# 80 of 100 term scatters moved to the experts' block, and the last score batch with its lane chain placed behind all expert tiles

## The chip, the cores and the metric

The kernel runs as one program on one core of a Trainium2 chip. The metric is the device time of one execution in microseconds. Three executions of the kernel before took 4361.23, 4351.35 and 4353.69 us; the median is 4353.69 us.

## What is computed

A graph layer and a routed expert layer over 12,500 nodes of 256 features, with 212,500 edges sorted by destination and 131,072 further edges for the router's attention. Cut to what matters:

```python
xn = layernorm(x)
x = x + gnn(xn, edges) + linear_attention(xn)         # gnn: mean of xn[src] per dst, then two matrices
h = layernorm(x) @ W_gat                              # 16 terms of each node (4 heads x 4 experts)
e = leaky_relu(a_src[src2] + a_dst[dst2])             # one score per head of each of 131072 edges + loops
ee = exp(e - segment_max(e, dst2)[dst2])
agg = segment_sum(h[src2] * ee / denom, dst2)         # softmax over the edges of a node
w = softmax(top2(mean_heads(layernorm(agg + b_gat)))) # two experts of each node
x = x + sum_e w[e] * (gelu(xn2 @ W1[e] + b1[e]) @ W2[e] + b2[e])
```

`xn2` is the layer norm of the new x. `a_dst`, four terms of each node, is what the moved scatters carry.

## The kernel before, in words

The program is four blocks, one after the other. At a block's end every engine meets the others at a barrier. The order inside a block is written out by hand: each engine has its own loop, and semaphores tie the loops together.

1. Loads of edges and weights.
2. A sort of the router's edges by destination across the 128 lanes (DVE), and the first layer norm beside it.
3. **The graph block** (L646 to L1120). GpSimd (POOL) gathers 128 rows at a time for 1664 chunks of edges (L796), and TensorE sums them by one-hot matrices. Beside it, a software pipeline over 100 tiles of 125 nodes makes the mean, the attention and the second layer norm of each tile, and last `router_row` (L936) copies each tile's router terms into `rt` (stored as `route_rows`) and its four destination terms into `ad_all`. After its last gather POOL scatters `ad_all`, one tile at a time (L799 to L802), into `ad_rows`: the terms of a node go to the place of its first edge.
4. **The experts' block** (L1122 on). TensorE runs 25 groups of 4 tiles: 32 products by W1 for the group into `HP` (L1587), a Gelu on ScalarE into `hid` (L1560), then 16 products by W2 per tile into `Y` (L1595). DVE adds the bias into `y_sb` (L1534), SyncE stores it to `y_rows` (L1223). Two `Y` buffers are in turn, so TensorE waits for DVE at `s_yc` two tiles later.

Beside the tiles runs the edge softmax, in 16 batches of 64 columns of 128 edges. POOL gathers `nb` (source terms, L1270, 64 a batch), at most `AHEAD` = 4 in flight and 3 batch buffers deep. Between two tiles DVE does `scores(b)` (L1309) after tile `unit_after(b)` and `records(b)` (L1334) after the tile behind that; ScalarE takes the exponentials; SyncE stores each batch of running records to `rec_rows` (L1226). Since a node's edges may run over from one lane to the next, the **lane chain** repairs the ends: `lane_ends`, `over_lanes`, `lane_sums`, `first_maxima`, `first_records` (L1355 to L1429). It needs two rounds of transposes on TensorE (L1601, L1606), two exponentials on ScalarE, one gather on POOL (`fix`, L1276, after the last record store) and one scatter back (L1279). The place of each part is a fixed number of tiles behind the last batch:

```python
def unit_after(b):
    t = int((b + 1) * 5.65) + 3
    return t if t % 4 < 2 else t + 4 - t % 4
```

This gives tiles 8, 16, 20, 25, 32, 36, 44, 48, 53, 60, 65, 72, 76, 84, 88 and 93 for the 16 batches, so `LAST` is 93 and the chain's five parts stand after tiles 94 to 98.

The kernel's **tail**: POOL gathers the last record of each node, 100 gathers `res` (L1286). `weigh(k)` makes the gates of 20 tiles on DVE (L1437 on), and `combine(t)` (L1520) sums the four expert rows of a tile, which SyncE has loaded from `y_rows` 8 tiles ahead (`final_loads`, L1240) and stores to `out` (L1250).

Of the kernel before, what the change touches and what calls it, by code (L numbers as in the profile page):

```python
# [8 lines left out]
ACT = mybir.ActivationFunctionType  # L9
# [4 lines left out]
NT = N // NP  # L14
# [33 lines left out]
FT = 20  # L48
FG = NT // FT
AHEAD = 4  # L50
NS = 2 * SPANS
MIX_AT = NT + 3
HISTS = FC // 8
# [66 lines left out]

def unit_after(b):

    t = int((b + 1) * 5.65) + 3
    return t if t % 4 < 2 else t + 4 - t % 4


def build(nc, x, src, dst, gnn_w, gnn_b, wqkv, wkv_t, wout_t, bout, w_gat, att_src, att_dst,
          b_gat, ln_g, ln_b, w1, b1, w2, b2, fedge, out):
    ctx = ExitStack()
    with ctx:  # L130
# [515 lines left out]
        with ExitStack() as stage, nc.Block() as block:  # L646
# [141 lines left out]
            @block.gpsimd  # L788
            def _(pool):
                nc.gpsimd.iota(spare[:], [[1, NP]], base=EF, channel_multiplier=NP, allow_small_or_imprecise_dtypes=True).then_inc(s_sp, 1)  # L790

                for s in range(NS):
                    g, h, w = s // 2, s % 2, s // 2 % 2
                    pool.wait_ge(s_used[h], g + 1)
                    for q in range(HU):
                        pool.indirect_dma_start(out=rows[w][h][:, q, 0:D], out_offset=None, in_=xn_rows,  # L796
                                                in_offset=bass.IndirectOffsetOnAxis(ap=gsrc[:, s * HU + q:s * HU + q + 1], axis=0)
                                                ).then_inc(s_rows[w][(h * HU + q) // QUAD], 16)
                for t in range(NT):  # L799
# [322 lines left out]
        with ExitStack() as stage, nc.Block() as block:  # L1122
# [78 lines left out]
            LAST = unit_after(NB - 1)  # L1201
            assert LAST + 4 < NT and LAST // 4 == NG - 2

            @block.sync
            def _(sp):
                for to, of in ((b1_sb[:], b1), (b2_b[:], row_of(b2.rearrange("e f -> (e f)"), NE * D)), (bg[:], row_of(b_gat, 16)),
                               (lg[:], row_of(ln_g, 16)), (lb[:], row_of(ln_b, 16))):
                    sp.dma_start(to, of).then_inc(s_pl, 16)

                def load_group(g):  # L1210
                    u = g % 2
                    if g >= 2:
                        sp.wait_ge(s_hp, (g - 1) * 16)
                    for i in range(4):
                        sp.dma_start(x2g[u][:, :, i, :], x2_turned[4 * g + i].rearrange("p (k n) -> p k n", k=2)).then_inc(s_x2l[u], 16)

                load_group(0)
                load_group(1)
                sp.wait_ge(s_ads, 16 * NT)
                sp.dma_start(ad[:], ad_rows[0:EF, :].rearrange("(p f) h -> p f h", p=P)).then_inc(s_adl, 16)  # L1220
                for t in range(NT):
                    sp.wait_ge(s_yc, t + 1)
                    sp.dma_start(y_rows[t], y_sb[t % 2][:]).then_inc(s_ys[t % 2], 16)  # L1223
                    for b in batches_after(t - 2):
                        sp.wait_ge(s_rec, b + 1)
                        sp.dma_start(rec_rows[0:EF, :].rearrange("(p f) c -> p f c", p=P)[:, b * W:(b + 1) * W, :],  # L1226
                                     rec[b % 2][:]).then_inc(s_recs[b % 2], 16)
                    if t % 4 == 0 and t // 4 + 2 < NG:
                        load_group(t // 4 + 2)

                def final_loads(t):
                    q = t % YR
                    if t % FT == 0:
                        k = t // FT
                        if k >= 2:
                            sp.wait_ge(s_mrg, k - 1)
                        sp.dma_start(own[k % 2][:], route_rows[t * NP:(t + FT) * NP, :].rearrange("(t p) c -> p t c", p=NP)).then_inc(s_own, 16)
                    if t >= YR:
                        sp.wait_ge(s_acc, t - YR + 1)
                    sp.dma_start(y_in[q], y_rows[t]).then_inc(s_yl[q], 16)  # L1240
                    sp.dma_start(x1_in[q], x1_rows[t]).then_inc(s_yl[q], 16)  # L1241

                sp.wait_ge(s_y, NT)
                for u in range(2):
                    sp.wait_ge(s_ys[u], 16 * NT // 2)
                for t in range(YR):
                    final_loads(t)
                for t in range(NT):
                    sp.wait_ge(s_acc, t + 1)
                    sp.dma_start(out[t * NP:(t + 1) * NP, :], acc[t % AR][:]).then_inc(s_out[t % AR], 16)  # L1250
                    if t + YR < NT:
                        final_loads(t + YR)
                for q in range(AR):
                    sp.wait_ge(s_out[q], 16 * NT // AR)

            @block.gpsimd
            def _(pool):
                nc.gpsimd.memset(first_e[:], 1.0).then_inc(s_fe, 1)
                pool.wait_ge(s_fe, 1)
                nc.gpsimd.affine_select(out=first_e[:], in_=first_e[:], compare_op=ALU.is_gt, fill=0.0, base=0,  # L1260
                                        pattern=[[1, 4], [-1, 4]], channel_multiplier=0).then_inc(s_fe, 1)
                pool.indirect_dma_start(out=ad_first[:], out_offset=None, in_=route_rows,
                                        in_offset=bass.IndirectOffsetOnAxis(ap=first_i[:, 0:1], axis=0)).then_inc(s_adf, 16)
                for b in range(NB):
# [25 lines left out]
            def _(dve):  # L1290
# [238 lines left out]
                for t in range(NT):  # L1529
                    dve.wait_ge(s_y, t + 1)  # L1530
                    if t >= 2:
                        dve.wait_ge(s_ys[t % 2], (t // 2) * 16)
                    for half in range(2):
                        last = v.tensor_tensor(y_sb[t % 2][0:NP, half * 512:half * 512 + 512], Y[t % 2][half][0:NP, :],  # L1534
                                               b2_b[:, half * 512:half * 512 + 512], ALU.add)
                    last.then_inc(s_yc, 1)
                    if t == unit_after(0) - 3:
                        start_ad()
                    for b in batches_after(t - 1):
                        records(b)  # L1540
                    for b in batches_after(t):
                        scores(b)
                    for part, at in ((lane_ends, 1), (over_lanes, 2), (lane_sums, 3), (first_maxima, 4), (first_records, 5)):
                        if t == LAST + at:
                            part()
                for k in range(FG):
                    weigh(k)
                    for t in range(k * FT, (k + 1) * FT):
# [3 lines left out]
            def _(act):  # L1552
                a = nc.scalar.activation
                act.wait_ge(s_pl, 5 * 16)
                for g in range(NG):
                    for c in range(16):
                        act.wait_ge(s_hp, g * 16 + c + 1)
                        if g:
                            act.wait_ge(s_y, g * 4)
                        a(hid[:, c, :], HP[c % 4][:, 0:4 * NP], ACT.Gelu, bias=b1_sb[:, c:c + 1]).then_inc(s_hid, 1)  # L1560
                    for j in range(4):
                        for b in batches_after(4 * g + j):
                            act.wait_ge(s_dif, b + 1)
                            a(dd[:], dd[:], ACT.Exp).then_inc(s_ex, 1)
                    if g == LAST // 4:
                        act.wait_ge(s_endd, 1)
                        a(dc[:], dc[:], ACT.Exp).then_inc(s_ende, 1)
# [11 lines left out]
            def _(pe):  # L1579
                mm = nc.tensor.matmul  # L1580
                def group(g, u, pair):
# [9 lines left out]
                    for j in range(4):  # L1591
# [6 lines left out]
                        if isinstance(g, int) and 4 * g + j == LAST + 2:  # L1598
                            pe.wait_ge(s_ends, 1)
                            for k in range(4):  # L1600
                                last = nc.tensor.transpose(HP[0][0:20, k * P:(k + 1) * P], ends[:, k, :], ident)  # L1601
                            last.then_inc(s_endt, 1)
                            pe.wait_ge(s_endc, 1)
                        if isinstance(g, int) and 4 * g + j == LAST + 3:
                            pe.wait_ge(s_fx, 1)
                            nc.tensor.transpose(HP[1][:, 0:20], fm[:, 0:P], ident[0:20, 0:20])  # L1606
                            nc.tensor.transpose(HP[1][:, 20:40], fx[:, 0:P], ident[0:20, 0:20]).then_inc(s_back, 1)

                for g in range(2):
                    group(g, g, 0)  # L1610
# [2 lines left out]
                        group(i * 2 + (2 + u), u, i + 1)  # L1613
                for g in range(NG - 3, NG):
                    group(g, g % 2, g // 2)


_INS = ["x", "src", "dst", "L0_gnn_weight", "L0_gnn_bias", "L0_mix_Wqkv", "kv_turned", "out_turned", "L0_mix_bout",
# [26 lines left out]
```

## Time and profile before

| | us |
|---|---|
| median of three executions | 4353.69 |
| lowest and highest | 4351.35, 4361.23 |
| the profiled execution, first to last instruction | 4353.6 |
| first instruction of the experts' block | 2548.7 |
| first gather of final records (`res`) | 3961.8 |

The profiled execution has no time of its own beside its span; the span lies 0.1 us from the median of the runs, so differences in it are differences of the metric.

| engine | busy us | share of the span |
|---|---|---|
| TensorE, products | 3225.6 | 74% |
| GpSimd | 2900.5 | 67% |
| VectorE | 2057.2 | 47% |
| ScalarE | 831.1 | 19% |

How to read it: a share is an average over four blocks with different limits. The table says who is busy, and only the waits inside a stage say what ends it. A time in a stage is read as the distance between two starts in the timeline, and the rows that are used stand in the section of rows.

### The profile page before, as it was taken

What the parts mean: (1) busy time and instruction counts of PE and PEld (TensorE: products, weight loads), DVE (VectorE), ACT (ScalarE), POOL (GpSimd) and SP (SyncE); (2) the same over time, 40 slices, a digit from 0 to 9 for tenths busy, and PEclk for the clock granted to TensorE, in tenths of its full rate; (3) what the DMA queues carried; (4) which work ended last, traced back from release to release, by engine and by line L of the source; (5) the groups of instructions that cost most, each with busy time, mean ns of one, the idle gap of its engine ahead of it and who ended that gap; (6) DMA issues with size and microseconds to landing.
All of it is one profiled execution on the core that took longest, in us unless ns stands there. A gap on an engine that the chain in (4) does not pass through costs nothing. (4 is left out here: it accounts for less than half of the span.)

```text
span 4353.6 us, 47649 instructions
## 1 busy us (share of the span) xinstructions
PE 3225.6 (74%) x12938; PEld 2167.4 (50%) x12938; DVE 2057.2 (47%) x4751; ACT 831.1 (19%) x2082; POOL 2900.5 (67%) x3009
## 2 busy tenths in 40 slices
PE   0118999999997788888888449999999999993000
PEld 0105666665655565555555326666666666662000
DVE  7885656555655465555455202122223223233677
ACT  4301222222221011111111112222222222221000
POOL 1617777777777777777777767777777777754210
PEclk6559999999999899998999779999999999997555
DMA  6205555555554577666666322222222222223766
GB/s 205 88 31 133 138 137 138 136 138 135 138 137 138 138 182 193 178 177 178 174 180 177 72 55 60 67 69 67 69 62 74 67 67 73 67 66 122 217 208 218
DMA packets 378974, 540.08 MB, mean 124 GB/s; under 512 B 117914, under 2 KB 295418, under 8 KB 378743
## 3 DMA queue, kind: packets, MB, share of 16 engines
q0 software_dynamic: 119136, 234.44, 23.8%
q1 hardware_dynamic: 259735, 304.59, 21.9%
q14 instruction: 78, 0.64, 0.0%
q8 instruction: 25, 0.41, 0.0%
HBM read 392.03 MB, written 146.74 MB: 124 GB/s over the span
## 5 line engine op out<-in xcount | busy, mean ns | idle before, releaser
L796 POOL DMA_INDIRECT rows<-xn_rows,gsrc x1664 | 1578.4, 949 | 507.5 <-issue 506.9
L1270 POOL DMA_INDIRECT nb<-route_rows,idx x1024 | 1014.9, 991 | 318.9 <-issue 302.9
L1024 PE MATMUL PS<-rows,oh 128*128 128x257 f32 x3328 | 884.6, 414 | 277.2 <-DMA rows<-xn_rows,gsrc 276.0
L1024 PEld LDWEIGHTS PS<-rows,oh 128*128 128x128 f32 x3328 | 645.7, 203 | 434.4 <-DMA rows<-xn_rows,gsrc 327.9
L1587 PE MATMUL PS<-x2g,arena 128*128 128x500 f32 x1600 | 678.4, 585 | 95.9 <-DMA x2g<-x_turned 94.1
L1595 PE MATMUL PS<-arena,hid 128*125 128x256 f32 x3200 | 697.5, 380 | 20.8 <-ACT hid L1560 20.8
L1595 PEld LDWEIGHTS PS<-arena,hid 128*125 128x125 f32 x3200 | 598.6, 188 | 129.4 <-issue 33.1
L1534 DVE TENSOR_TENSOR y_sb<-PS,b_b 125x512 f32<-125x512 f32 x200 | 128.6, 685 | 1058.1 <-PE PS L1595 1057.7
L1587 PEld LDWEIGHTS PS<-x2g,arena 128*128 128x128 f32 x1600 | 305.2, 191 | 455.0 <-issue 357.2
L1560 ACT ACTIVATE hid<-PS,b_sb 128x500 f32<-128x500 f32 x400 | 270.8, 677 | 615.8 <-PE PS L1587 615.8
L836 DVE TENSOR_TENSOR oh<-PS,rel 128x1024 f32<-128x1024 f32 x208 | 253.9, 1221 | 11.0
L849 DVE TENSOR_REDUCE ss<-sq 125x16 f32<-125x1024 f32 x100 | 122.0, 1220 | 250.7 <-ACT sq L974 250.7
L1096 PE MATMUL PS<-own_w,p_t 128*125 128x512 f32 x400 | 222.7, 640 | 10.5 <-ACT s_t L984 10.5
L629 PE MATMUL PS<-wide,arena 128*128 128x128 f32 x112 | 27.6, 428 | 248.9 <-DVE arena L545 203.5
L1041 PE MATMUL PS<-arena,x_t 128*125 128x512 f32 x400 | 193.2, 605 | 0.0
L1043 PE MATMUL PS<-arena,x_t 128*125 128x512 f32 x400 | 188.0, 592 | 0.0
L1286 POOL DMA_INDIRECT res<-rec_rows,end_i x100 | 98.7, 987 | 111.2 <-DVE q L1454 80.1
L866 DVE TENSOR_TENSOR oh_lo<-PS,arena 128x500 bf16<-128x500 f32 x256 | 170.9, 667 | 0.0
L866 DVE TENSOR_TENSOR oh_hi<-PS,arena 128x400 bf16<-128x400 f32 x256 | 144.4, 564 | 53.2 <-PE PS L1059 52.9
L973 ACT ACTIVATE sq<-PS 125x512 f32<-125x512 f32 x100 | 59.7, 597 | 540.3 <-PE PS L1043 540.3
L441 POOL TENSOR_SCALAR space<-space,nm,rs 128x256 f32<-128x256 f32 x98 | 104.5, 1083 | 84.5 <-DVE rs L512 84.5
L1520 DVE SCALAR_TENSOR_TENSOR acc<-arena,gate,acc 125x256 f32<-125x256 f32 x300 | 145.5, 485 | 24.3 <-issue 2.2
(300 smaller groups left out, 3122.5 us busy)
## 6 DMA issues: line engine op xcount, KB each, us to landing
y_rows<-y_sb SPq DMA_DIRECT2D x100, 512.0 KB, 2.7
arena<-y_rows SPq DMA_DIRECT2D x100, 512.0 KB, 5.0
rows<-xn_rows,gsrc POOLq DMA_INDIRECT x1664
nb<-route_rows,idx POOLq DMA_INDIRECT x1024
sum_rows<-kept SPq DMA_DIRECT2D x104, 128.5 KB
x_rows<-x SPq DMA_DIRECT2D x100, 128.0 KB, 4.8
hid<-x_rows SPq DMA_DIRECT2D x100, 128.0 KB, 8.3
m_in<-sum_rows SPq DMA_DIRECT2D x100, 125.5 KB
```

The costliest lines, as they stand in the source:

```text
L796: pool.indirect_dma_start(out=rows[w][h][:, q, 0:D], out_offset=None, in_=xn_rows, in_offset=bass.IndirectOffsetOnAxis(ap=gsrc[:, s * HU + ...
L836: v.tensor_tensor(oh[w][h][:], NUMBERS.rearrange("p (o n) -> p o n", o=1).broadcast_to([P, HU, P]), along(rel[h][:], P), ALU.is_equal).the ...
L866: last = v.tensor_tensor(to[:, 4 * h:4 * h + 4, :], NUMBERS[:, 0:n].rearrange("p (o n) -> p o n", o=1).broadcast_to([P, 4, n]), along(of[: ...
L1024: last = mm(SUM[:, 0:D + 1], oh[w][h][:, q, :], rows[w][h][:, q, :], start=h == 0 and q == 0, stop=h == 1 and q == HU - 1)
L1041: mm(KP[0:NP, :], x_t[u][:, k * NP:(k + 1) * NP], wkv[:, k, 0:INNER], start=k == 0, stop=k == 1)
L1043: last = mm(VP[u][0:NP, :], x_t[u][:, k * NP:(k + 1) * NP], wkv[:, k, INNER:2 * INNER], start=k == 0, stop=k == 1)
L1096: both = lambda k: mm(GM[u][0:NP, :], p_t[q][:, k * NP:(k + 1) * NP], own_w[:, k, :], start=k == 0, stop=k == 1)
L1270: pool.indirect_dma_start(out=nb[b % NBUF][:, c, :], out_offset=None, in_=route_rows, in_offset=bass.IndirectOffsetOnAxis(ap=idx[:, b * W ...
L1520: last = v.scalar_tensor_tensor(out=acc[t % AR][:], in0=y_in[q][0:NP, e * D:(e + 1) * D], scalar=gate[:, t, e:e + 1], in1=acc[t % AR][:] i ...
L1560: a(hid[:, c, :], HP[c % 4][:, 0:4 * NP], ACT.Gelu, bias=b1_sb[:, c:c + 1]).then_inc(s_hid, 1)
L1587: last = mm(HP[c % 4][:, 0:4 * NP], w1_sb[:, k, e, (c % 4) * P:(c % 4 + 1) * P], x2g[u][:, k, :, :].rearrange("p j n -> p (j n)"), start=k ...
L1595: last = mm(Y[j % 2][e // 2][0:NP, (e % 2) * D:(e % 2 + 1) * D], hid[:, 4 * e + k, j * NP:(j + 1) * NP], w2_sb[:, e, k, :], start=k == 0, ...
```

## The change

Three things change together.

The scatters are split at `ADS_EARLY` = 20: 20 stay in the graph block, 80 go to the front of POOL's program in the experts' block, ahead of `ad_first` and of all `nb` gathers. SyncE's load of `ad`, which needs all 100, moves from before tile 0 to behind the store of tile 6. `start_ad` goes by `unit_after(0) - 3`, from tile 5 to tile 9.

`unit_after` gives tiles 12, 17, 24, 29, 36, 41, 48, 53, 60, 68, 72, 80, 84, 92, 96 and 100: the last batch stands behind all tiles, and is called `late`.

The lane chain follows the late batch with nothing between its parts, on DVE, ScalarE and TensorE. SyncE stores the late records behind the first eight `final_loads`.

```diff
+ADS_EARLY = 20
 def unit_after(b):
-    t = int((b + 1) * 5.65) + 3
-    return t if t % 4 < 2 else t + 4 - t % 4
+    t = int((b + 1) * 6.06 + 5.5)
+    t = t if t % 4 < 2 else t + 4 - t % 4
+    return min(t, NT)
...
-                for t in range(NT):
+                for t in range(ADS_EARLY):
                     pool.wait_ge(s_hc, t + 2)
                     pool.indirect_dma_start(out=ad_rows, ...)
...
-                sp.wait_ge(s_ads, 16 * NT)
-                sp.dma_start(ad[:], ad_rows[0:EF, :]...).then_inc(s_adl, 16)
                 for t in range(NT):
                     sp.wait_ge(s_yc, t + 1)
                     sp.dma_start(y_rows[t], y_sb[t % 2][:]).then_inc(s_ys[t % 2], 16)
                     for b in batches_after(t - 2):
+                        store_records(b)
+                    if t == 6:
+                        sp.wait_ge(s_ads, 16 * NT)
+                        sp.dma_start(ad[:], ad_rows[0:EF, :]...).then_inc(s_adl, 16)
...
                 for t in range(YR):
                     final_loads(t)
+                for b in late:
+                    store_records(b)
...
+                for t in range(ADS_EARLY, NT):
+                    pool.indirect_dma_start(out=ad_rows, ...).then_inc(s_ads, 16)
                 pool.indirect_dma_start(out=ad_first[:], ...)
...
-                    for part, at in ((lane_ends, 1), (over_lanes, 2), ...):
-                        if t == LAST + at:
-                            part()
+                for b in late:
+                    scores(b)
+                    records(b)
+                lane_ends()
+                over_lanes()
+                lane_sums()
+                first_maxima()
+                first_records()
```

ScalarE's exponentials and TensorE's transposes of the chain move behind the last group in the same way.

How POOL's program reads at the boundary of the two blocks (`ad_rows` are the scatters, `nb` the gathers of source terms), before:

```order
L796 DMA rows<-xn_rows,gsrc 128x256 x7
L801 DMA ad_rows<-ad_all,start_i 143872x4 [waits s_hc] x100
L646 UNCONDITIONAL_BRANCH
L1256 UNCONDITIONAL_BRANCH [waits barrier_Pool_Activation_PE_DVE_SP_gather]
L1258 MEMSET first_e 125x16
L1260 AFFINE_SELECT first_e<-first_e 125x16 [waits s_fe]
L1262 DMA ad_first<-route_rows,first_i 128x28
L1270 DMA nb<-route_rows,idx 128x28 x4
```

and in the changed kernel:

```order
L798 DMA rows<-xn_rows,gsrc 128x256 x7
L803 DMA ad_rows<-ad_all,start_i 143872x4 [waits s_hc] x20
L648 UNCONDITIONAL_BRANCH
L1265 UNCONDITIONAL_BRANCH [waits barrier_Pool_Activation_PE_DVE_SP_gather]
L1267 MEMSET first_e 125x16
L1269 AFFINE_SELECT first_e<-first_e 125x16 [waits s_fe]
L1272 DMA ad_rows<-ad_all,start_i 143872x4 x80
L1274 DMA ad_first<-route_rows,first_i 128x28
L1282 DMA nb<-route_rows,idx 128x28 x4
```

Of the 100 scatters ahead of the barrier 20 are left, and 80 stand between the barrier and the first gather of the batches.

TensorE's program at the lane chain (`x2g` rows are products by W1, `hid` rows products by W2, `ends`, `fm` and `fx` the chain's transposes), before:

```order
L1595 MATMUL PS<-arena,hid 125x256 [waits s_yc]
L1595 MATMUL PS<-arena,hid 125x256 x15
L1601 MATMUL PS<-wide,ends 20x128 [waits s_ends]
L1601 MATMUL PS<-wide,ends 20x128 x3
L1587 MATMUL PS<-x2g,arena 128x500 [waits s_hid,s_x2l0,s_endc]
L1587 MATMUL PS<-x2g,arena 128x500
...
L1595 MATMUL PS<-arena,hid 125x256 [waits s_yc,s_hid]
L1595 MATMUL PS<-arena,hid 125x256 x15
L1606 MATMUL PS<-wide,fm 128x20 [waits s_fx]
L1607 MATMUL PS<-wide,fx 128x20
L1595 MATMUL PS<-arena,hid 125x256 [waits s_yc]
```

and the end of the changed kernel's:

```order
L1614 MATMUL PS<-arena,hid 125x256 [waits s_yc]
L1614 MATMUL PS<-arena,hid 125x256 x15
L1614 MATMUL PS<-arena,hid 125x256 [waits s_yc]
L1614 MATMUL PS<-arena,hid 125x256 x15
L1627 MATMUL PS<-wide,ends 20x128 [waits s_ends]
L1627 MATMUL PS<-wide,ends 20x128 x3
L1631 MATMUL PS<-wide,fm 128x20 [waits s_fx,s_endc]
L1632 MATMUL PS<-wide,fx 128x20
```

The two rounds of transposes stood between groups and tiles of the experts, with waits on the chain's semaphores. Now nothing of the experts stands behind them.

SyncE's program behind the last tiles (`y_rows<-y_sb` stores a tile, `arena<-y_rows` and `hid<-x_rows` are the final loads), before:

```order
L1223 DMA y_rows<-y_sb 128x1024 [waits s_yc] x5
L1226 DMA rec_rows<-rec 128x1536 [waits s_rec]
L1223 DMA y_rows<-y_sb 128x1024 [waits s_yc] x4
L1237 DMA own<-route_rows 125x20x28 [waits s_ys1,s_ys0,s_y]
L1240 DMA arena<-y_rows 128x1024
L1241 DMA hid<-x_rows 128x256
L1240 DMA arena<-y_rows 128x1024
```

and in the changed kernel:

```order
L1224 DMA rec_rows<-rec 128x1536 [waits s_rec]
L1229 DMA y_rows<-y_sb 128x1024 [waits s_yc]
L1244 DMA own<-route_rows 125x20x28 [waits s_ys1,s_ys0,s_y]
L1247 DMA arena<-y_rows 128x1024
L1248 DMA hid<-x_rows 128x256
...
L1247 DMA arena<-y_rows 128x1024
L1248 DMA hid<-x_rows 128x256
L1224 DMA rec_rows<-rec 128x1536 [waits s_rec]
L1259 DMA out<-acc 125x256 [waits s_acc]
```

The last store of records has moved from between the tile stores to behind 17 loads.

## Rows read from the trace of the kernel before

**Rows 1.** A stretch at the end of the graph block; PE, PEld, DVE, ACT, POOL busy, clock, DMA, GB/s.

```profile
2480.00:2500.00 20.00, 0.00 (x0) 0.00 (x0) 0.00 (x0) 0.00 (x0) 15.23 (x16) 0.50 0.03 2
```

**Rows 2.** The scatters, line L801: duration ns min/median/max, first and last start.

```profile
L801 POOL DMA_INDIRECT ad_rows<-ad_all,start_i x100: 965/970/1147, 2411.9 to 2538.3; - x100
```

**Rows 3.** Timeline across the experts' barrier: start, duration, engine, what, [idle before].

```profile
2538.30 0.97 POOL L801 DMA_INDIRECT ad_rows<-ad_all,start_i  x1 [0.30 <-issue]
2548.74 0.11 POOL L1258 MEMSET first_e<- 125x16 f32 x1 [9.47 <-POOLq L646]
...
2560.03 2.87 PE L1587 MATMUL PS<-x2g,arena 128*128 128x500 f32 x3 [94.12 <-DMA x2g<-x_turned]
```

**Rows 4.** Waits of SyncE's queue: total us, times, longest.

```profile
SPq L646 <- PEq L646: 80.3, 1, 80.3
```

**Rows 5.** Timeline across the barrier ahead of the graph block.

```profile
324.05 0.16 DVE L586 TENSOR_TENSOR lane<-lane 128x1 f32<-128x1 f32 x1
...
325.51 0.25 POOL L790 IOTA spare<- 100x125 f32 x1 [86.23 <-POOLq L381]
```

**Rows 6.** The gathers of source terms, line L1270, whole block.

```profile
L1270 POOL DMA_INDIRECT nb<-route_rows,idx x1024: 939/945/4119, 2550.8 to 3883.4; - x171
```

**Rows 7.** POOL's waits from 2549 to 2600 us.

```profile
POOL nb L1270 <- DMA nb<-route_rows,idx: 5.2, 3, 2.8
```

**Rows 8.** SyncE's queue: last record store, first and last of the 17 first final loads.

```profile
3903.40 0.43 SPq L1226 DMA_DIRECT2D rec_rows<-rec  x1
...
3968.26 0.29 SPq L1237 DMA_DIRECT2D own<-route_rows  x1
...
3981.87 0.43 SPq L1241 DMA_DIRECT2D hid<-x_rows  x1
```

**Rows 9.** The first 20 gathers of final records, beside those loads.

```profile
DMA to landing us min/median/max: 2.4/4.5/6.6
```

**Rows 10.** DVE's timeline from the last batch to the end of the lane chain.

```profile
3885.93 0.17 DVE L1316 COPY m_run<-m_run 128x4 f32<-128x4 f32 x1 [3.52 <-DMA nb<-route_rows,idx]
...
3894.93 5.32 DVE L1349 TENSOR_TENSOR_SCAN rec<-dd,rec,msg 128x64 f32<-128x64 f32 x20
...
3902.93 0.67 DVE L1379 COPY endt<-PS 20x512 f32<-20x512 f32 x1
...
3906.38 0.28 DVE L1394 TENSOR_SCALAR dc<-dc 20x256 f32<-20x256 f32 x1
...
3941.93 0.27 DVE L1398 TENSOR_TENSOR dc<-dc,endt 20x128 f32<-20x128 f32 x1
...
3951.59 0.19 DVE L1405 COPY back<-PS 128x40 f32<-128x40 f32 x1
...
3953.26 0.17 DVE L1420 TENSOR_TENSOR d<-z 128x8 f32<-128x8 f32 x1
...
3958.49 0.17 DVE L1426 TENSOR_TENSOR fix<-fix,d 128x20 f32<-128x20 f32 x1
```

**Rows 11.** TensorE's timeline: the chain's two rounds of transposes.

```profile
3900.81 1.03 PE L1601 MATMUL PS<-wide,ends 128*20 128x128 f32 x4 [5.91 <-DVE ends L1363]
...
3942.95 0.23 PE L1606 MATMUL PS<-wide,fm 20*128 20x20 f32 x1 [2.26 <-DVE fx L1401]
```

**Rows 12.** POOL's timeline behind its last gather of source terms.

```profile
3908.32 0.95 POOL L1276 DMA_INDIRECT fix<-rec_rows,fix_i  x1 [23.99 <-DMA rec_rows<-rec]
3959.29 0.99 POOL L1279 DMA_INDIRECT rec_rows<-fix,put_i  x1 [50.02 <-DVE fix L1429]
3961.81 0.97 POOL L1286 DMA_INDIRECT res<-rec_rows,end_i  x1 [1.53 <-DMA rec_rows<-fix,put_i]
```

**Rows 13.** DVE's timeline: the first instruction of the tail.

```profile
3990.77 0.24 DVE L1437 TENSOR_TENSOR zf<-res,own 125x80 f32<-125x80 f32 x1 [25.28 <-DMA res<-rec_rows,end_i]
```

**Rows 14.** The chain that ended last, one group of tiles: start us, us, what.

```profile
2617.18 26.84 PE PS L1587 x64
2644.77 27.89 PE PS L1595 x128
```

More of the change, by code:

```diff
@@ L1200, in build @@
             batches_after = lambda t: [b for b in range(NB) if unit_after(b) == t]
-            LAST = unit_after(NB - 1)
-            assert LAST + 4 < NT and LAST // 4 == NG - 2
+            late = batches_after(NT)
+            assert len(late) == 1
             @block.sync
@@ L1218, in _, with store_records @@
                 load_group(1)
-                sp.wait_ge(s_ads, 16 * NT)
-                sp.dma_start(ad[:], ad_rows[0:EF, :].rearrange("(p f) h -> p f h", p=P)).then_inc(s_adl, 16)
+                def store_records(b):
+                    sp.wait_ge(s_rec, b + 1)
+                    sp.dma_start(rec_rows[0:EF, :].rearrange("(p f) c -> p f c", p=P)[:, b * W:(b + 1) * W, :],
+                                 rec[b % 2][:]).then_inc(s_recs[b % 2], 16)
                 for t in range(NT):
@@ L1224, in _ @@
                     for b in batches_after(t - 2):
-                        sp.wait_ge(s_rec, b + 1)
-                        sp.dma_start(rec_rows[0:EF, :].rearrange("(p f) c -> p f c", p=P)[:, b * W:(b + 1) * W, :],
-                                     rec[b % 2][:]).then_inc(s_recs[b % 2], 16)
+                        store_records(b)
+                    if t == 6:
+                        sp.wait_ge(s_ads, 16 * NT)
+                        sp.dma_start(ad[:], ad_rows[0:EF, :].rearrange("(p f) h -> p f h", p=P)).then_inc(s_adl, 16)
                     if t % 4 == 0 and t // 4 + 2 < NG:
@@ L1261, in _ @@
                                         pattern=[[1, 4], [-1, 4]], channel_multiplier=0).then_inc(s_fe, 1)
+                for t in range(ADS_EARLY, NT):
+                    pool.indirect_dma_start(out=ad_rows, out_offset=bass.IndirectOffsetOnAxis(ap=start_i[:, t:t + 1], axis=0),
+                                            in_=ad_all[:, t, :], in_offset=None).then_inc(s_ads, 16)
                 pool.indirect_dma_start(out=ad_first[:], out_offset=None, in_=route_rows,
@@ L1542, in _ @@
                         scores(b)
-                    for part, at in ((lane_ends, 1), (over_lanes, 2), (lane_sums, 3), (first_maxima, 4), (first_records, 5)):
-                        if t == LAST + at:
-                            part()
+                for b in late:
[6 more added lines that the diff above has]
+                first_records()
                 for k in range(FG):
@@ L1564, in _ @@
                             a(dd[:], dd[:], ACT.Exp).then_inc(s_ex, 1)
-                    if g == LAST // 4:
-                        act.wait_ge(s_endd, 1)
-                        a(dc[:], dc[:], ACT.Exp).then_inc(s_ende, 1)
+                for b in late:
+                    act.wait_ge(s_dif, b + 1)
+                    a(dd[:], dd[:], ACT.Exp).then_inc(s_ex, 1)
+                act.wait_ge(s_endd, 1)
+                a(dc[:], dc[:], ACT.Exp).then_inc(s_ende, 1)
                 act.wait_ge(s_fixd, 1)
@@ L1597, in group @@
                         last.then_inc(s_y, 1)
[L1598 to L1607, printed above, removed]
                 for g in range(2):
@@ L1615, in _ @@
                     group(g, g % 2, g // 2)
+                pe.wait_ge(s_ends, 1)
+                for k in range(4):
+                    last = nc.tensor.transpose(HP[0][0:20, k * P:(k + 1) * P], ends[:, k, :], ident)
+                last.then_inc(s_endt, 1)
+                pe.wait_ge(s_endc, 1)
+                pe.wait_ge(s_fx, 1)
+                nc.tensor.transpose(HP[1][:, 0:20], fm[:, 0:P], ident[0:20, 0:20])
+                nc.tensor.transpose(HP[1][:, 20:40], fx[:, 0:P], ident[0:20, 0:20]).then_inc(s_back, 1)
 _INS = ["x", "src", "dst", "L0_gnn_weight", "L0_gnn_bias", "L0_mix_Wqkv", "kv_turned", "out_turned", "L0_mix_bout",
```

## The prediction, made before the run

> **What bounds the kernel now.** I read the stretch by stretch table first, then the timelines at the seams, and last the waits. Three stages matter.
>
> The end of the graph block: from 2480 to 2500 us only GpSimd works [rows 1]. The 100 scatters, 2411.9 to 2538.3 [rows 2], end that block alone, and the next block's first instruction starts at 2548.74 [rows 3]. SyncE had arrived and waited 80.3 us at the barrier [rows 4]: it was ready at 2548.7 - 80.3 = 2468.4.
>
> The experts' block: two engines run nearly equal courses. TensorE takes 26.84 us and 27.89 us for the two halves of a group, and the halves start 27.56 apart [rows 14], so a group takes 55.6 us and 25 of them some 1390. GpSimd's 1024 gathers start from 2550.8 to 3883.4 [rows 6]. The last batch lands at 3885.93 [rows 10], so the course is 1.30 us a gather and 83.4 a batch. The first gather of final records is at 3961.81 [rows 12]. Of the 75.9 us between, most is no work: GpSimd waits 50.02 us for the end of the lane chain [rows 12], whose parts wait in VectorE's order for tiles 95 to 98.
>
> The tail, from 3961.81 to 4353.6, is 391.8 us. It starts with the final records, so it moves with them.
>
> **The change part by part.** Each term is what it adds to the time at which the final records can be gathered.
>
> 1. *The block starts earlier.* Of 100 scatters 20 stay: from 2411.9 at 1.277 us each (126.4 us over 99 steps [rows 2]) they end at 2437, long before SyncE's 2468.4. SyncE then ends the block. What does the barrier cost? Across the barrier before the graph block, the last VectorE instruction ends at 324.21 and GpSimd starts at 325.51 [rows 5]: 1.3 us. At the experts' barrier there are 9.5 us between the last scatter's end and the start [rows 3]. I take 1.3, since in both cases the late engine is then not GpSimd with scatters just issued, and GpSimd's own 9.5 us would be over by 2447. The block starts at 2469.7 instead of 2548.74: **-79.0**. With the other price it is -70.8; that end is kept.
>
> 2. *80 scatters stand ahead of the gathers.* 80 x 1.277 = **+102.1**. They wait for nothing: the terms have been in `ad_all` since the graph block. Queued behind them are `ad_first` and all gathers, and behind those VectorE's batches. The new table has been set for that: batch b has landed 104.2 + 83.4(b+1) us into the block, for batch 7 at 771; its scores stand after tile 53, which ends at 11.3 (first product at 2560.03 [rows 3]) + 13 x 55.6 + 28 + 14 = 776 [rows 14]. The even places have 20 us or more. So VectorE does not stand waiting with a `Y` buffer in hand. The load of `ad` behind tile 6 (about 117 us into the block) finds the scatters landed at about 107. No term. A batch buffer is free three batches later as before: no term.
>
> 3. *Start-up waits.* The first gathers waited 5.2 us [rows 7] beside the block's first loads. Scatters don't wait for landings; the 2 MB load of `ad` now meets gathers later, for some 2 us. **-3**, between -5.2 and 0.
>
> 4. *The final loads now run beside the last gathers.* TensorE no longer stops for the chain (5.91 + 2.26 us of waits and 1.3 of transposes [rows 11], some 10), so the loads, first issued at 3968.26 [rows 8], start at 3968.3 - 79.0 - 10 = 3879. The 17 are issued in 13.6 us, and their 5 MB need about 26 at the 200 GB/s that the tail moves on the page. The last gather lands near 3908, so 22 gathers or so run beside them. Before, the first gathers of final records ran beside these loads and landed in 2.4 / 4.5 / 6.6 us [rows 9]. With four in flight and 1.25 us apart, a landing up to 5.0 us costs nothing; 6.6 makes it 1.7 us a gather, +10 for the 22. I take **+2**, nearest to the median row, and keep 0 and +10.
>
> The trace has just this pairing in rows 9, so the sum goes by it. The Trainium skill (DMA: Bandwidth & Descriptors, Queues, rings and completion order) says that each DMA engine goes round robin between its queue rows and changes only after a whole packet. By that rule every gather waits behind packets of the loads, which speaks for the +10 and not for the +2; the largest landing agrees with it, the median doesn't decide.
>
> 5. *The chain has nothing between its parts.* From the rows: last landing to the end of the record scans 3900.25 - 3885.93 = 14.3, less 0.6 for a tile's bias that stood in it, 13.7 [rows 10]; to the end of the transposes at 3901.84, 1.6 [rows 11]; `endt` copy to the lane differences 3902.93 to 3906.66, 3.7 [rows 10]; an exponential (0.5, an estimate) and the sums with transposes 3941.93 to 3943.18, 1.8 together [rows 10, 11]; `first_maxima` 3951.59 to 3953.43, 1.85 [rows 10]; an exponential of 0.3 and `first_records` up to GpSimd's scatter, 3958.49 to 3959.29, 0.8 [rows 10, 12]; scatter to first gather 2.5 [rows 12]. Together 26.3, with handovers 27. Before it was 75.9: **-48.9**. The other branch, record store then `fix` gather, takes 4.9 us from the store's issue at 3903.40 [rows 8] to the gather at 3908.32 [rows 12], and 2.4 for a landing [rows 9], 7.3; VectorE needs it 8 us after the scans, so it is covered by under a microsecond, if SyncE is past its 17 loads (issued by 3893, needed at 3922). TensorE's transposes now come after idle time at the low clock; that is 1.03 us of work [rows 11], at most +1.5.
>
> 6. *The tail.* The first `weigh` started 28.96 us after the first gather, since the 20th landed late beside the loads [rows 9, 12, 13]. Now the loads are over; 19 x 1.25 + 2.4 = 26.2: **-2.8**. Behind it the transfers set the pace as before: 0.
>
> Sum: -79.0 + 102.1 - 3 + 2 - 48.9 - 2.8 = **-29.6**. From the execution's 4353.6 that is **4324.0 us**; its span lies 0.1 from the median of the runs, so no correction. The two big gains are bought with the scatters: what is won is the exposed boundary and the slack in the chain.
>
> **The rivals.** A measurement here tells 0.2%, 8.7 us, from no change.
>
> *A: the boundary keeps its 9.5 us* because it is a price of this barrier and not of the scatters. For it: it is the only row of this barrier. Against: rows 5. 4324.0 + 8.2 = 4332.
>
> *B: the last gathers crawl beside the loads.* +8 over my term: 4332; still faster. A and B together, with landings above 6.6 us, 4324 + 8.2 + 14 = 4346: within 0.2%.
>
> *C: the chain doesn't shrink.* Its place is between the last landing and the first final record. If its steps are bound by latencies that overlapped with tiles in the trace (table loads, the record store behind 17 loads, handovers), the 75.9 us stay, and the sum is -29.6 + 48.9 = +19.3: 4373, slower. It decides from a chain of 27 + 29.6 = 57 us; slower by over 0.2% from 65. Against it: 34 us of it are one wait of VectorE for a tile, between the end at 3906.66 and the tile's bias ahead of 3941.93 [rows 10].
>
> *D: the block doesn't start earlier*, since another engine holds the barrier: +79, 4403. Rows 4 nearly exclude it.
>
> **How the numbers follow.** My forecast 0.58; A alone 0.16; B alone 0.10; A and B with slow landings 0.08; C 0.07; D 0.01. Faster 0.58 + 0.16 + 0.10 = 0.84; same 0.08; slower 0.07 + 0.01 = 0.08. The range goes from 4314 (start-up waits gone, B's term 0, the chain 5 shorter) to 4342 (A with B), and leaves out C, D and A with slow landings, 0.16.
>
> **What would show it.** The experts' block starts near 2470 and GpSimd's 80 scatters take 102 us. The last gather lands near 3908, 34 us behind TensorE's last product. The final records start 27 us after it, near 3935. The tail is 389 us. Wrong would be: a start near 2478 (A), waits of `nb` for landings behind the last tile (B), a chain above 35 us (C), or waits of VectorE for `nb` between tiles that push TensorE past GpSimd.

## The result, and the profile after

The changed kernel takes 4322.17 us (4316.73 to 4324.76), the kernel before 4353.69 (4351.35 to 4361.23). The ratio is 0.9927, with a 95% interval of 0.9914 to 0.9939: faster by 0.7%. The prediction was 4324.0 us, in a range of 4314 to 4342. The profiled execution took 4322.32 us with a span of 4320.5, so 33.1 us of span are gone; the times of its stages are used below. In every execution on record that has both, the time is 1.7 to 1.9 us above the span. So the profiled execution before, with its span of 4353.6, took some 4355.4 us and not the median, and the forecast of 4324.0, summed up from that span, is a span too: as a time it is 4325.8.

| us, profiled execution | before | after | predicted |
|---|---|---|---|
| first instruction of the experts' block | 2548.74 | 2464.08 | 2469.7 |
| last batch landed | 3885.93 | 3905.94 | 3908 |
| landing to first final record | 75.9 | 26.4 | 27 |
| first final record | 3961.81 | 3932.29 | 3935 |
| from there to the end | 391.8 | 388.2 | 389 |

First the seam of the two blocks, which answers to [rows 3]: the timeline from 2461 us on; the columns are start, duration, engine, line, what, and the idle time before it. SyncE's wait at the barrier, which answers to [rows 4], stands behind it.

```profile
2461.69 0.16 DVE L945 COPY rt<-PS 125x8 f32<-125x8 f32 x1
2464.08 0.11 POOL L1267 MEMSET first_e<- 125x16 f32 x1 [24.36 <-POOLq L648]
...
2464.79 0.99 POOL L1272 DMA_INDIRECT ad_rows<-ad_all,start_i  x1 [0.30 <-issue]
```

```profile
SPq L648 <- PEq L648: 0.2, 1, 0.2
```

GpSimd now waits 24.36 us at the barrier, and VectorE with SyncE behind it ends the block: VectorE's last instruction ends at 2461.85, SyncE waits only 0.2 us, and the next block starts 2.2 us after VectorE's end. Then come the 80 scatters and the gathers (the rows of lines L1272 and L1282; durations in ns, first and last start):

```profile
L1272 POOL DMA_INDIRECT ad_rows<-ad_all,start_i x80: 968/972/990, 2464.8 to 2565.6; - x80
```

```profile
L1282 POOL DMA_INDIRECT nb<-route_rows,idx x1024: 942/947/3502, 2568.2 to 3903.5; - x171
...
  issue: 302.3, 990
  DMA nb<-route_rows,idx: 19.5, 34
```

From the first scatter to `ad_first` at 2566.90 it is 102.1 us, and no wait is among them. The end of the batches, the chain and the start of the tail, in order of time, answer to [rows 8, 10, 11, 12]:

```profile
3865.33 1.29 DVE L1546 TENSOR_TENSOR y_sb<-PS,b_b 125x512 f32<-125x512 f32 x2 [3.69 <-PE PS L1614]
...
3869.38 0.29 SPq L1244 DMA_DIRECT2D own<-route_rows  x1
...
3905.94 0.17 DVE L1328 COPY m_run<-m_run 128x4 f32<-128x4 f32 x1 [39.33 <-DMA nb<-route_rows,idx]
...
3914.20 5.32 DVE L1361 TENSOR_TENSOR_SCAN rec<-dd,rec,msg 128x64 f32<-128x64 f32 x20
3919.55 0.32 SPq L1224 DMA_DIRECT2D rec_rows<-rec  x1
...
3920.08 1.03 PE L1627 MATMUL PS<-wide,ends 128*20 128x128 f32 x4 [54.79 <-DVE ends L1375]
...
3921.14 0.68 DVE L1391 COPY endt<-PS 20x512 f32<-20x512 f32 x1
...
3923.53 1.27 POOL L1288 DMA_INDIRECT fix<-rec_rows,fix_i  x1 [19.05 <-DMA rec_rows<-rec]
...
3925.39 0.28 DVE L1410 TENSOR_TENSOR dc<-dc,endt 20x128 f32<-20x128 f32 x1 [0.48 <-ACT dc L1586]
```

VectorE has nothing to do for 39.33 us ahead of the last batch, and after it the chain runs with no wait of VectorE above 0.6 us. The waits of GpSimd in the stretch from 3900 us to the tail:

```profile
POOL fix L1288 <- DMA rec_rows<-rec: 19.1, 1, 19.1
...
POOL rec_rows L1291 <- DVE fix L1441: 5.0, 1, 5.0
POOL res L1298 <- DMA rec_rows<-fix,put_i: 1.4, 1, 1.4
```

The 50.02 us that it waited for `fix` in [rows 12] are 5.0 now. In those 5.0 us VectorE is still at work on the sums, so its branch, and not the `fix` gather, is the one that ends last.

### The profile page after: what moved, and what is told of

Read it like the earlier page. It is cut to its first block and busy times, and to the rows that moved or that the text cites. A ratio compares the mean times of both kernels' runs of the same rounds, so it can differ in the third digit from the quotient of the medians.

```text
span 4320.5 us, 47644 instructions
## 1 busy us (share of the span) xinstructions
PE 3219.4 (75%) x12936; PEld 2165.2 (50%) x12938; DVE 2063.0 (48%) x4751; ACT 826.0 (19%) x2078; POOL 2904.4 (67%) x3009
## 5 line engine op out<-in xcount | busy, mean ns | idle before, releaser
L1282 POOL DMA_INDIRECT nb<-route_rows,idx x1024 | 1014.8, 991 | 321.8 <-issue 302.3
L1614 PEld LDWEIGHTS PS<-arena,hid 128*125 128x125 f32 x3200 | 598.6, 188 | 129.5 <-issue 33.1
```

Source lines behind the costliest of these rows:

```text
L1282: pool.indirect_dma_start(out=nb[b % NBUF][:, c, :], out_offset=None, in_=route_rows, in_offset=bass.IndirectOffsetOnAxis(ap=idx[:, b * W ...
```

## The experiments

Each edit is against the changed kernel, where not said otherwise. A time is the median of the runs, a ratio is to the kernel before on the same chip. Each edit of `ADS_EARLY` alone keeps the new table of places.

**The new chain without the moved scatters.** All 100 scatters stay ahead of the barrier.

```diff
-ADS_EARLY = 20
+ADS_EARLY = 100
```

> The changed kernel with all 100 scatters back in the graph block; the new table, the late batch and the chain behind all tiles stay. Theory P (GpSimd's course and the last tile, whichever ends later, set the chain's start): the experts' block starts at 2548.7 as before, its last gather lands 1339.8 us later at 3888.5 (3905.94 - 2568.20 + 2.1 by the changed kernel's trace), but the last tile's bias ends 1402.5 us into the block, at 3951.2. The chain takes 26 us from there and its record store now runs behind and beside the final loads, some 10 more; the tail is 388. Time 4366 to 4376, slower than before by 12 to 22 us. Rival Q (the close-packed chain is a gain of its own, 49 us, wherever the scatters stand): 4353.7 - 48.9 = 4305.

Measured: 4378.34 us, ratio 1.006 (1.0043 to 1.0077), slower than before. GpSimd and VectorE around the block's end, the last batch and the chain (the timeline):

```profile
2539.89 0.97 POOL L803 DMA_INDIRECT ad_rows<-ad_all,start_i  x1 [0.30 <-issue]
2550.33 0.11 POOL L1267 MEMSET first_e<- 125x16 f32 x1 [9.47 <-POOLq L648]
...
3953.57 0.16 DVE L1328 COPY m_run<-m_run 128x4 f32<-128x4 f32 x1
...
3980.89 0.94 POOL L1288 DMA_INDIRECT fix<-rec_rows,fix_i  x1 [94.29 <-DMA rec_rows<-rec]
...
3985.77 1.00 POOL L1291 DMA_INDIRECT rec_rows<-fix,put_i  x1 [3.94 <-DVE fix L1441]
3988.21 0.97 POOL L1298 DMA_INDIRECT res<-rec_rows,end_i  x1 [1.45 <-DMA rec_rows<-fix,put_i]
```

GpSimd's last `nb` gather is at 3885.4, and then the batch lies for some 66 us until the last tile is through VectorE, since its place is behind all tiles. The first final record comes 1437.9 us into the block, where it came after 1413.1 in the kernel before. So the late places and the late chain by themselves cost 0.6%, and the time lies above the 4366 to 4376 expected. They pay only if the gathers end late in the block; no run here has the new table and the close chain apart, so their shares stay open.

**The moved scatters without the new places and chain.** The kernel before, split at 20, with the load of `ad` behind the store of tile 4.

```diff
-                for t in range(NT):
+                for t in range(ADS_EARLY):
...
+                for t in range(ADS_EARLY, NT):
+                    pool.indirect_dma_start(out=ad_rows, ...)
```

> The kernel before with the 80 scatters moved and nothing else, save that the load of ad stands behind the store of tile 4 (its first user comes at tile 5). Theory P: block starts at 2464, the last gather lands at 3906 as in the changed kernel, VectorE stands waiting for every batch and holds the tiles back, so the chain keeps its 75.9 us behind the last landing: final records at 3982, tail 389 to 392, time 4371 to 4374, slower than before by 17 to 20 us. Rival R (the earlier start is the gain, and the scatters' place hides itself): at least -79 + 26 and so 4322 or less.

Measured: 4373.3 us, ratio 1.005 (1.0033 to 1.0067). The block started at 2459.4, and yet it was slower. The waits from 2600 to 3990 us (in all, times, longest):

```profile
DVE m_run L1321 <- DMA nb<-route_rows,idx: 115.0, 9, 23.9
POOL rec_rows L1284 <- DVE fix L1434: 50.7, 1, 50.7
...
PE PS L1600 <- DVE y_sb L1539: 44.8, 3, 28.0
...
DVE m_run L1324 <- DMA nb<-route_rows,idx: 34.0, 1, 34.0
```

VectorE stands at 10 of its 16 places before the batch has landed (the wait for the first batch has a row of its own, 34.0 us), TensorE then runs out of `Y` buffers, and the chain keeps its 50.7 us. Neither half of the change gains; the 0.7% come from both together.

**All scatters behind the barrier.**

```diff
-ADS_EARLY = 20
+ADS_EARLY = 0
```

> The changed kernel with all 100 scatters in the experts' block. Theory P: block starts at 2460 to 2466, the last gather lands 20 x 1.277 = 25.5 us later than in the changed kernel; VectorE now waits 15 to 21 us for each batch at an odd place (tiles 17, 29, 41, 53), which pushes the last tile from 3867 to some 3888, still before the last landing at 3931. Time 4322.2 + 25.5 = 4347.7. Rival S (GpSimd's course does not set the end): 4322 if transfers do, about 4343 if the tiles do and their push of 21 us counts.

Measured: 4346.58 us, ratio 0.9989 (0.9979 to 0.9998). Each of the 20 scatters is worth 24.4 / 20 = 1.22 us against the changed kernel. VectorE waited for `nb` at five places, from 2600 us on, and 2.8 us more at the first batch:

```profile
DVE m_run L1328 <- DMA nb<-route_rows,idx: 99.1, 5, 50.7
```

Of these 99.1 us, 50.7 are the last place; the other four push the tiles 13 us later (the last bias ends 1415.9 us into the block, in the changed kernel 1402.5). That costs nothing, since the bias is done at 3875.0 and the last batch lands at 3925.7.

**30 scatters ahead of the barrier.**

```diff
-ADS_EARLY = 20
+ADS_EARLY = 30
```

> The changed kernel with 30 scatters in the graph block and 70 in the experts' block. Theory P: 30 scatters end at 2414.3 + 30 x 1.277 = 2452.6, and with 9.5 us on top at 2462.1, still before the others' 2461.9 to 2464; the block starts at 2464, the last gather lands 12.8 us earlier, at 3893.2, still 26 behind the last tile. Time 4322.2 - 12.8 = 4309.4. Rival S (the tiles or the final transfers set the end of the changed kernel): no change from 4322.

Measured: 4311.18 us, ratio 0.9906 (0.9889 to 0.9922), 11 us less than the changed kernel for 10 scatters; 12.8 was expected. In the profiled executions the last batch lands 1431.2 us into the block instead of 1441.9, and the chain takes the same 26.4 us. So it is GpSimd's course of scatters and gathers that sets the end here.

**46 scatters ahead.**

```diff
-ADS_EARLY = 20
+ADS_EARLY = 46
```

> The changed kernel with 46 scatters in the graph block. They end at 2414.3 + 46 x 1.277 = 2473.0, after all others, so GpSimd holds the barrier. If the barrier then costs 9.5 us as before (price of scatters just issued): start 2482.5, last landing 2482.5 + 1408.7 = 3891.2, last tile 3885, time 4307. If it costs 1.3 us (the 9.5 was something else): start 2474.3, last landing 3883.0, last tile 3876.8, time 4299. Rival S (end not set by GpSimd's course): 4322 or later, by the later start of the tiles 4333 to 4341.

Measured: 4304.48 us, ratio 0.9892 (0.9875 to 0.9908). GpSimd is the last at the barrier again, and SyncE waits 15.9 us there. The price is neither 1.3 nor 9.5:

```profile
2467.57 0.97 POOL L803 DMA_INDIRECT ad_rows<-ad_all,start_i  x1 [0.30 <-issue]
2474.91 0.11 POOL L1267 MEMSET first_e<- 125x16 f32 x1 [6.37 <-POOLq L648]
...
2475.19 0.91 DVE L1537 MEMSET y_sb<- 128x1024 f32 x1 [18.47 <-PEq L648]
...
3895.16 0.43 SPq L1224 DMA_DIRECT2D rec_rows<-rec  x1
...
3905.53 0.94 POOL L1288 DMA_INDIRECT fix<-rec_rows,fix_i  x1 [31.44 <-DMA rec_rows<-rec]
```

The tiles' course is now as late as the gathers': the last bias starts at 3876.9, the scores at 3878.15 without a wait, and the chain takes 34.8 us instead of 26.4. The interval overlaps with that of 30 scatters, so the two are not told apart.

**Is the block end's price the landing of scatters?** The kernel before, with a wait for all scatters and a mark behind it.

```diff
                     pool.indirect_dma_start(out=ad_rows, ...).then_inc(s_ads, 16)
+                pool.wait_ge(s_ads, 16 * NT)
+                nc.gpsimd.memset(spare[:, 0:1], 0.0)
```

> The kernel before, with a wait of GpSimd for the landing of all 100 scatters at the end of the graph block, and a one-column memset behind it as a mark. Asks what the 9.5 us between the last scatter and the experts' block are. Theory L (they are the scatters' landing, which the barrier waits for anyhow): the mark stands where the landing is, near 2547, and the block starts 1.3 us behind it. Theory G (an end-of-block price of GpSimd after it has issued transfers, not their landing): the mark stands 2 to 3 us after the last scatter, near 2541.5, and the block starts 6 to 8 us behind the mark; time 4352 to 4355, no change. A third way: the wait lets that price run out beside it, block start near 2543, time 4346 to 4348.

Measured: 4353.69 us, ratio 1.0003 (0.9994 to 1.0013). The timeline at the mark:

```profile
2537.33 0.10 POOL L804 MEMSET spare<- 100x1 f32 x1 [1.19 <-DMA ad_rows<-ad_all,start_i]
2546.90 0.11 POOL L1260 MEMSET first_e<- 125x16 f32 x1 [9.47 <-POOLq L646]
...
2547.18 0.91 DVE L1527 MEMSET y_sb<- 128x1024 f32 x1 [91.67 <-PEq L646]
```

The last scatter has landed before the mark at 2537.33, and the 9.47 us begin behind it all the same. So it is no wait for the scatters' data: it belongs to the end of GpSimd's part of the block.

**What sets that price?** Two kernels of one execution each, with 72 and with 54 scatters ahead.

```diff
-ADS_EARLY = 20
+ADS_EARLY = 72
```

> The change with ADS_EARLY = 72, one look at the barrier: what sets the time from GpSimd's last scatter to the next block? It was 9.47 with 100 scatters (before, e1) and 6.37 with 46 (e4). Theory W (it grows with the number of GpSimd's instructions left in the stretch that it works alone): straight between them, 6.37 + 26/54 x 3.1 = 7.9. Rival X (two levels, 9.47 once the other engines have sat idle long enough, 6.37 before): 9.47 or 6.37. Block start near 2410 + 71 x 1.277 + 1 + 7.9 = 2509.6; time about 4304 + 33 = 4337 to 4342.

```diff
-ADS_EARLY = 20
+ADS_EARLY = 54
```

> The same with ADS_EARLY = 54, the second point. Theory W: 6.37 + 8/54 x 3.1 = 6.8. Rival X: 9.47 or 6.37. Block start near 2410 + 53 x 1.277 + 1 + 6.8 = 2485.5; time about 4304 + 10 = 4314.

Measured, with 72: 4341.32 us; with 54: 4318.07 us. The barrier's waits with 72, then with 54:

```profile
DVE y_sb L1537 <- PEq L648: 46.6, 1, 46.6
...
POOL first_e L1267 <- POOLq L648: 8.5, 1, 8.5
```

```profile
DVE y_sb L1537 <- PEq L648: 28.3, 1, 28.3
...
POOL first_e L1267 <- POOLq L648: 7.3, 1, 7.3
```

With 46, 54, 72 and 100 scatters the price is 6.37, 7.32, 8.49 and 9.47 us. Two levels are excluded. It grows, by 0.12 us a scatter at first and 0.04 at last, so a straight line is not right either. VectorE waited 18.5, 28.3, 46.6 and 82.8 us beside it, so in these four alone the price could as well go by the time that GpSimd works alone. Two pairs with the same number of scatters tell the two apart. The last run below has 46 again, and VectorE waited 7 us less there:

```profile
2473.99 0.11 POOL L1267 MEMSET first_e<- 125x16 f32 x1 [6.37 <-POOLq L648]
...
2474.28 0.91 DVE L1537 MEMSET y_sb<- 128x1024 f32 x1 [11.58 <-PEq L648]
```

The price is 6.37 us in both. With 100 scatters VectorE waited 81.3, 82.8 and 91.7 us (the new chain alone, the kernel before, the landing wait), and the price is 9.47 us in all three. So it goes with the number of scatters ahead of the barrier or with what grows in step with it, such as the time since the last gather, and not with the time that the other engines wait; by which mechanism stays open.

**38 scatters ahead.**

```diff
-ADS_EARLY = 20
+ADS_EARLY = 38
```

> The change with ADS_EARLY = 38. Times by the number left behind: 0: 4346.6, 20: 4322.2, 30: 4311.2, 46: 4304.5. Theory P: each scatter is worth 1.28 us until GpSimd itself holds the barrier, 6.4 us behind its last scatter (e4); 38 scatters end at 2410 + 48.5 = 2458.5, plus 6.4 is 2465, so the barrier is still free of them, and the gathers come 8 x 1.277 = 10.2 us earlier than with 30: 4301, unless the last tile comes first: by e4 the last tile ends near 3877.5 and the batches of 38 would land near 3881, so little is lost there and 4301 to 4304 is expected. Rival F (flat optimum: the last tile and the chain beside the loads set the end from about 36 on): 4304 to 4306, as e4.

Measured: 4294.50 us, ratio 0.9865 (0.9848 to 0.9881): the best version, 1.35% under the kernel before and nearly twice the gain of the change, and below both theories. Its interval just touches that of 46 scatters, but no execution of the one (4292.9 to 4295.9) comes near those of the other (4303.8 to 4304.9). GpSimd at the barrier, and VectorE and GpSimd at the end:

```profile
2456.02 0.97 POOL L803 DMA_INDIRECT ad_rows<-ad_all,start_i  x1 [0.30 <-DVE rt L945]
2464.89 0.11 POOL L1267 MEMSET first_e<- 125x16 f32 x1 [7.91 <-POOLq L648]
...
3867.36 1.29 DVE L1546 TENSOR_TENSOR y_sb<-PS,b_b 125x512 f32<-125x512 f32 x2 [3.70 <-PE PS L1614]
...
3878.35 0.17 DVE L1328 COPY m_run<-m_run 128x4 f32<-128x4 f32 x1 [9.70 <-DMA nb<-route_rows,idx]
...
3895.92 1.29 POOL L1288 DMA_INDIRECT fix<-rec_rows,fix_i  x1 [19.95 <-DMA rec_rows<-rec]
```

The block starts 2.24 us after VectorE's last instruction (which ends at 2462.65), as in the changed kernel, so GpSimd's price is hidden. The last batch lands at 3878.35, where with 46 the scores also start (3878.15); but the tiles end 9.6 us earlier, so the final loads are issued from 3871.4 on, and all have been issued when the late record store is given at 3891.95. That store then lands in time, and the chain takes 26.4 us. With 46 the loads begin at 3881.4, and the store, behind them in SyncE's queue, was issued at 3895.16 and held up the `fix` gather until 3905.53.

That the gain was larger than 10.2 us from 30 to 38 has one part that rows show: most gathers are through before the final loads start. GpSimd's waits for landings from 3865 us on are 4.7 us in the changed kernel, 4.6 with 30 scatters, and here

```profile
POOL nb L1282 <- DMA nb<-route_rows,idx: 0.5, 1, 0.5
```

The rest of the step of 16.7 us is not shown. The profile with 30 scatters is of the slowest of its four executions (4320.59 us), and its block started 5.5 us later than here.

**The final loads behind the late record store**, at 20 and at 46.

```diff
-                for t in range(YR):
-                    final_loads(t)
                 for b in late:
                     store_records(b)
+                for t in range(YR):
+                    final_loads(t)
```

> The changed kernel with the 17 first final loads issued behind the late record store, so nothing runs beside the last gathers. My term 4 (+2 us, waits of 4.2 us in the changed trace behind 3870): the last landing comes 3 to 4 us earlier, and the first weigh starts 28 to 29 us after the first final gather instead of 26.2, since the loads now stand there. Time 4321 to 4324, within 2 us of 4322.2. Rival B (round robin between queue rows makes the last gathers crawl): last landing 8 to 10 us earlier, time 4315 to 4317.

Measured: 4323.97 us, ratio 0.9931 (0.9915 to 0.9948), no gain. GpSimd's late waits fell from 4.7 to 0.5 us, and the last 24 steps from gather to gather from 33.0 to 30.0 us, which is what they took in the kernel before. The last batch landed 1440.2 us into the block instead of 1441.9; 3 to 4 us had been expected. But now the loads run beside the chain. GpSimd's waits there:

```profile
POOL rec_rows L1291 <- DVE fix L1441: 5.7, 1, 5.7
POOL res L1298 <- DMA rec_rows<-fix,put_i: 5.1, 1, 5.1
```

The landing of the scatter back costs 5.1 us instead of 1.4, and the chain 31.1 instead of 26.4. The loads cost 3.0 us beside the gathers and 4.7 beside the chain, so the gathers are the cheaper place. Four gathers are in flight there and the chain's transfers are in flight alone, which would explain it; no run varies that number.

> The change with ADS_EARLY = 46 and, as in e6, the final loads behind the late store of records. In e4 the last batch waited for nothing but the last tile (scores at 3878.1), and from there to the first final record it was 34.8 us instead of the 26.4 of the changed kernel: the fix gather waited 31.4 us for the record store, which stands behind 17 loads that had just been issued. Theory Q (the queue of SyncE in front of the store is what lengthens this chain): the fix gather comes 17 to 20 us behind the start of the scores instead of 27, the final records about 6 us earlier, and the first weigh stays some 27 to 30 us behind them since the loads now run beside the final gathers: 4297 to 4301. Rival V (VectorE's part sets the chain, the store is covered): 4304 as e4, or up to 4308, since the loads come later and the tail waits for them.

Measured: 4302.17 us, ratio 0.9885 (0.9868 to 0.9901), against 0.9892 (0.9875 to 0.9908) for e4: no difference that counts. The store is ahead, and `fix` comes at 3897.72, 18.3 us behind the scores, as theory Q said. But from `fix` to the first final record it is 12.8 us instead of 7.4, beside the loads. What was won ahead of `fix` was nearly all given back behind it.

## Why the prediction was right

1. *The block starts earlier*: -79.0 predicted, -84.7 measured. The term that was most off in size is this one, by 5.7 us. 4.4 of these are in the graph block, not at the barrier: its last VectorE instruction ends at 2461.85 instead of 2466.25, and I had taken the old place for fixed. The rest is the barrier. I had put 1.3 us behind SyncE's arrival at 2468.4. But that arrival was already 2.15 us behind VectorE's last instruction, and in the changed kernel the whole way from that instruction to the new block is 2.2, of which SyncE waits 0.2. That GpSimd's own price would be over by then was right, and so rival A is out; e5 shows that it is a price of GpSimd's end and not of the landing, e1, e4, e5, e8, e10 and e11 that it goes with the number of scatters, and e9 that it hides under the other engines. That the term came within 5.7 us is in part luck: VectorE's end in that block lies between 2455.5 and 2469.3 in the thirteen profiles.

2. *80 scatters ahead*: +102.1 predicted, 102.1 measured. VectorE waited for `nb` at no place but the last, so the table was late enough. e2 and e7 show what stands on the other side: waits at 10 and at 6 places.

3 and 4. *Waits for landings*: -3 and +2 predicted, together -1. Measured, the first ones went from 5.2 to 4.5 us, -0.7, and those beside the final loads from nothing to 4.7. The last batch lands 1441.9 us into the block, where it was 1337.2: 104.7 more, 102.1 of it scatters, so +2.6. The loads are +3.0 of it, by the last 24 steps (33.0 us against 30.0 in the kernel before and in e6), for the +2 said. They also began earlier than I had said, at 3869.4 and not at 3879: beside the earlier block, the tiles' course is 14.3 us shorter (the last bias ends 1402.5 us into the block, not 1416.8), where I had counted 10 for the chain's stops. Rival B (+8 over the term) is out. The round robin of the Trainium skill (DMA: Bandwidth & Descriptors, Queues, rings and completion order) had spoken for the +10. The runs agree with it in the direction, since landings beside the loads are longer (5.1 us of wait against 1.4 in e6), but not in that sum: GpSimd waited 4.7 us for landings beside the loads, and their course became 3.0 us longer.

5. *The chain*: -48.9 predicted, 75.9 - 26.4 = -49.5 measured. Its steps came as read from [rows 10, 11, 12]: 13.6 us to the end of the scans (13.7 said), 1.6 to the end of the transposes, 3.8 to the lane differences. TensorE's transposes took 1.03 us as before: the granted clock was 0.50 of full speed, the lower level of 1.2 GHz, at these four in both kernels, so the up to 1.5 us that I had allowed for a lower clock had no ground. Rival C is out for this kernel, and e2, where the chain stays in its old places, kept 76.5 us from the last landing to the first final record and took 4373.3 us. That is C's time, but not its mechanism: 50.7 us of it are GpSimd's wait while the chain's parts stand between tiles. The covered branch (record store, `fix`, 7.3 us) held because the loads were past (the store landed in 3.2 us); in e4 and e1 they were not (9.6 us in e4), and the chain was 34.8 and 34.6 us. I had named this condition and given it no price: it is 8 us.

6. *The tail*: -2.8 predicted, -3.6 measured. The first gates wait 26.2 us for the 20th record as said; the rest is 0.8 us behind it, which the runs don't account for; the same tail takes 388.2 to 393.7 us in the thirteen profiles.

The terms measured are -84.7 + 104.7 - 49.5 - 3.6 = -33.1 us, against -29.6 predicted, so each main term held in sign and nearly in size. The misses partly cancel: -5.7 at the block's start stands against +3.6 in the landings. The median fell by only 31.5, because the profiled execution before lay 1.7 us above its median; what stands ahead of the prediction took its span for its time. Span with span the forecast is 3.5 us off, and not the 1.8 that 4324.0 beside 4322.17 suggests.

What stays open: why the graph block's other engines end at other times in each execution (below), and why GpSimd's price at the block's end grows with the scatters ahead of it.

## What to carry to other kernels

Where two engines run courses of nearly equal length, count how far behind the other each ends: work that follows the later one directly should have its place there, and work moved from an exposed seam onto a course with slack elsewhere pays only as far as that slack goes. Neither half of this change gained alone, so a pair of edits that shift the same balance must be costed as one. Then turn the number that sets the balance: 20, 30, 38 and 46 gave 0.9927, 0.9906, 0.9865 and 0.9892, and the best of these four lies just before the moved work becomes the last at the barrier and the loads begin to meet the chain.

## What the runs showed of the hardware

GpSimd with indirect transfers just issued ends its part of a block with 6.37 to 9.47 us in which it does nothing that the trace shows, growing with the number of scatters from 46 to 100: twice 6.37 with 46 and three times 9.47 with 100, however long the other engines had waited. This is not the landing (e5). It cost nothing with 38 scatters, where VectorE ended 5.7 us after the last one (e9).

The end of the graph block moves by itself: VectorE's last instruction there ended at 2466.25 in the profiled execution before, at 2461.85 after, and at 2455.5 in e5 (2547.18 less the 91.67 us that it waited), where nothing ahead of it was changed; in e1, with all 100 scatters too, at 2469.3. One execution gives a term that hangs on this end no closer than some 14 us.

The same landing costs differently by what else is in flight: beside the final loads the overlapped gathers lost 3.0 us over 24 steps (33.0 against 30.0 in e6), while the single scatter at the end of the chain lost 3.7 (5.1 against 1.4 us of wait).
